# Decayed keys and queries by GpSimd, the first norm's sum kept in PSUM, and the keys' bias from eight more columns of the queries' product

## What is computed

```python
# tokens: softmax over the n = 16 pixels of a window, per head (8 heads of 8)
q = _ln(reduce_feats, ln_q_w, ln_q_b) @ Wq.T
kv = _ln(unf, ln_kv_w, ln_kv_b) @ Wkv.T
attn = softmax(einsum('bhpd,bhpnd->bhpn', q * scale, k), axis=-1)
aggre = einsum('bhpn,bhpnd->bhpd', attn, v)
h = reduce_feats + aggre @ proj_w.T + proj_b
# linear attention in chunks of 128 tokens, carried state S
scores = einsum('bhcd,bhed->bhce', qi, ki) * mask
intra = einsum('bhce,bhed->bhcd', scores, vi)
inter = einsum('bhcd,bhde->bhce', qi * q_dec, S)
S_new = blk * S + einsum('bhcd,bhce->bhde', ki * k_dec, vi)
# first norm over the 64 channels
h = _layernorm(h + attention(h))
```

## Time and profile before

| | us |
|---|---|
| median of three runs | 2586.48 (2584.95 to 2589.83) |
| the profiled execution, its own time | 2589.41 |
| its span | 2587.0 |
| first block's last norm starts (L929) | 2164.7 |

### The profile page before, as it was taken

One profiled execution on the slowest core, in us unless ns is written; L12 is line 12 of the kernel. 1 busy time (PEld: TensorE's weight loads), 2 busy tenths in 40 slices (PEclk: granted clock), 3 DMA queues, 4 the chain that ended last, 5 costly groups with the idle time before them and its releaser, 6 DMA issues. The chain is left out here.

```text
span 2587.0 us, 91002 instructions
## 1 busy us (share of the span) xinstructions
PE 2248.5 (87%) x32685; PEld 1057.8 (41%) x32685; DVE 2053.0 (79%) x3996; ACT 1851.1 (72%) x4405; POOL 1839.2 (71%) x1949
## 2 busy tenths in 40 slices
PE   1888898888888888888888888888888885999997
PEld 1344444444444444444444444444444442222222
DVE  4588888887888888888888888888888886777775
ACT  2877777777777777777777777777777773555554
POOL 3688788887888888888888888888888862233333
PEclk9999999999999999999999999999999996999999
DMA  4433333333333333333333333333333300010001
GB/s 79 83 67 67 66 66 66 67 66 57 64 67 67 67 67 67 67 67 67 67 67 67 67 67 67 67 67 67 67 67 67 67 2 1 17 23 22 20 20 29
DMA packets 573783, 147.92 MB, mean 57 GB/s; under 512 B 573504, under 2 KB 573504, under 8 KB 573504
## 3 DMA queue, kind: packets, MB, share of 16 engines
q1 hardware_dynamic: 573504, 143.53, 29.0%
HBM read 135.10 MB, written 8.39 MB: 55 GB/s over the span
## 5 line engine op out<-in xcount | busy, mean ns | idle before, releaser
L709 POOL TENSOR_TENSOR pv<-vs,aw 128x512 f32<-128x512 f32 x512 | 540.2, 1086 | 306.5 <-DVE aw L912 306.5
L856 DVE TENSOR_TENSOR kqs<-ps,qqT 128x512 f32<-128x512 f32 x512 | 354.1, 692 | 299.5 <-PE ps L393 295.2
L595 ACT ACTIVATE xd<-xb 128x512 f32<-128x512 f32 x512 | 585.4, 1178 | 0.0
L388 PE MATMUL ps<-xb,w_ckv 64*64 64x512 f32 x2048 | 555.6, 619 | 5.0 <-DVE kqs L856 5.0
L393 PE MATMUL ps<-xb,w_ckv 64*64 64x512 f32 x2048 | 555.6, 619 | 0.0
L577 ACT ACTIVATE sqs<-ps 128x512 f32<-128x512 f32 x512 | 308.4, 602 | 247.2 <-PE ps L393 246.9
L753 POOL TENSOR_TENSOR xt<-xb 128x512 f32<-128x512 f32 x256 | 325.8, 1273 | 23.0 <-issue 22.6
L716 POOL TENSOR_TENSOR pv<-pv 128x512 f32<-128x512 f32 x256 | 320.5, 1271 | 0.0
L867 DVE TENSOR_TENSOR sm<-ps,decay 128x1024 f32<-128x1024 f32 x256 | 299.5, 1208 | 4.4 <-PE ps L471 4.4
L415 PE MATMUL ps<-w_ckv,xd 64*64 64x64 f32 x16384 | 301.1, 223 | 0.0
L415 PEld LDWEIGHTS ps<-w_ckv,xd 64*64 64x64 f32 x16384 | 266.1, 136 | 33.1 <-issue 3.0
(11 more groups left out here) (223 smaller groups left out, 4261.6 us busy)
## 6 DMA issues: line engine op xcount, KB each, us to landing
xb<-in_x_dram SPq DMA_DIRECT2D x512, 256.0 KB, 4.4
out_dram<-outb SPq DMA_DIRECT2D x128, 64.0 KB, 1.6
w1p<-in_L_ffn_w_dram SPq DMA_DIRECT2D x16, 16.0 KB
w2p<-in_L_ffn_w_dram SPq DMA_DIRECT2D x8, 16.0 KB
b1p<-in_L_ffn_b_dram SPq DMA_DIRECT2D x8, 0.2 KB
b2v<-in_L_ffn_b_dram SPq DMA_DIRECT2D x8, 2.0 KB
sm<-in_L_tok_Wkv_dram SPq DMA_DIRECT2D x4, 16.0 KB, 2.0
w_av<-in_L_attn_w_qkv_dram SPq DMA_DIRECT2D x4, 16.0 KB, 2.1
```

What stands on the lines that cost most here:

```text
L388: nc.tensor.matmul(KB[own, :], w_ckv[own, 2 * P + m * C:2 * P + (m + 1) * C], xv[own, j], start=True, stop=True)
L595: nc.scalar.activation(xd[:, j, :].rearrange("p (b t) -> p b t", b=ST), xb[:, f, :].rearrange("p (b t d) -> p d b t", b=ST, d=ST)[:, j], A ...
L709: nc.gpsimd.tensor_tensor(pv[:, at].rearrange("p (k d) -> p k d", d=D), vs[:, s, at].rearrange("p (k d) -> p k d", d=D), aw[:, j * W4:(j + ...
L856: V.tensor_tensor(kqs[:, j, :].rearrange("p (t d) -> p t d", d=ST), KB.rearrange("p (t d) -> p t d", d=ST), qqT[:, s, :].unsqueeze(2).to_b ...
```

## The change

Three things, in the first block alone.

1. `kd` and `qdm` are made by GpSimd, behind `htok` and ahead of the sums of x, and no more by VectorE.
2. The sum `lt` stays in PSUM, as `LT`, 144 columns of bank B5 where L518's product lies: VectorE adds `htok` in place, ScalarE squares it there. The norm into `h1` is one product of 144 columns that reads `LT`; it stands right behind `q2` and waits for `oT`. L518 now waits for `h1`, and `attend(0)` waits for ScalarE's squares and no more for the sum. `sblk` stands ahead of the sum.
3. The keys' bias comes from the queries' product: `w_qc` has eight more columns, VectorE scales them by `yrs` and adds `cb_row` into `sbq`, which has four slots, twice behind `q2`. TensorE's product with `selbk` in `turned` is gone. `mx` and `mxb` are two columns of bank B4 in place of SBUF.

The diff's core:

```diff
-                                nc.tensor.transpose(SB[:, d * P:(d + 1) * P], sv[:, d, :], ident[:])
-                            nc.tensor.matmul(sgr[:, :, 25:26], qqT[:, o, :], selbk[:], start=True,
-                                             stop=True).then_inc(tr_pe, 1)
+                                mm = nc.tensor.transpose(SB[:, d * P:(d + 1) * P], sv[:, d, :], ident[:])
+                            mm.then_inc(tr_pe, 1)
...
-                                mm = nc.tensor.matmul(B67[:, m, 0:P], h1[own, 4 * i + r + 1, 0:P], w_qc[own, :],
+                                mm = nc.tensor.matmul(B67[:, m, 0:P + HEADS], h1[own, 4 * i + r + 1, 0:P], w_qc[own, :],
...
-                            pe.wait_ge(lt_done, done(i, r, 5, 1))
+                            pe.wait_ge(ln_sq, done(i, r, 5, 1))
...
+                            pe.wait_ge(h1_done, done(i, r, 5, 1))
+                            nc.tensor.matmul(LT, oT[:], w_ap[:], start=True, stop=True).then_inc(pr_done, 1)
...
+                        if s == 1:
+                            pool.wait_ge(st_ev, pairs(i, r, 0, 2))
+                            pool.wait_ge(s_pe, pairs(i, r, -1))
+                            nc.gpsimd.tensor_tensor(kd[:].rearrange("p (m h d) -> p m h d", m=2, d=D),
+                                                    kpl[:].rearrange("p (m h d) -> p m h d", m=2, d=D),
+                                                    kdec[:].unsqueeze(1).unsqueeze(3).to_broadcast([P, 2, HEADS, D]),
+                                                    ALU.mult).then_inc(kd_done, 1)
+                        else:
+                            pool.wait_ge(o_done, done(i, r, 5, 1))
+                            nc.gpsimd.tensor_tensor(qdm[:], qT[:, o, :], qdec[:], ALU.mult).then_inc(qd_done, 1)
...
                         V.tensor_tensor(heads(q2[:]), B67[:, :, 0:C], yrs[:, 2:4, 2:3].to_broadcast([P, 2, C]),
-                                        ALU.mult).then_inc(q2_done, 1)
+                                        ALU.mult)
+                        for m in range(2):
+                            ins = V.scalar_tensor_tensor(sbq[:, (r + 1) % 4, m * HEADS:(m + 1) * HEADS],
+                                                         B67[:, m, P:P + HEADS], yrs[:, 2 + m, 2:3],
+                                                         cb_row[:, m * HEADS:(m + 1) * HEADS], ALU.mult, ALU.add)
+                        ins.then_inc(q2_done, 1)
+                    if there(i, r, 5):
+                        dve.wait_ge(oT_done, done(i, r, 4, 1))
+                        V.tensor_tensor(h1[:, bass.ds(4 * i + r - 5, 1), :].rearrange("p o (m c) -> p (o m) c", c=CR),
+                                        LT.rearrange("p (m c) -> p m c", c=CR),
+                                        yrs[:, 0:2, 2:3].to_broadcast([P, 2, CR]), ALU.mult).then_inc(h1_done, 1)
...
-                        for m in range(2):
-                            ins = V.tensor_scalar(h1[:, bass.ds(4 * i + r - 5, 1), m * CR:(m + 1) * CR],
-                                                  lt[:, m * CR:(m + 1) * CR].unsqueeze(1), yrs[:, m, 2:3], None, ALU.mult)
-                        ins.then_inc(h1_done, 1)
...
-                        V.tensor_tensor(lt[:], B5[:, P:P + 2 * CR], htok[:, s, :], ALU.add).then_inc(lt_done, 1)
...
+                        V.tensor_tensor(LT, LT, htok[:, s, :], ALU.add).then_inc(lt_done, 1)
```

More of the change, by code:

```diff
@@ L98, in vit_tower_kernel @@
         B5 = ps[:, 5, :]
+        LT = B5[:, P:P + 2 * CR]
         B6 = ps[:, 6, :]
@@ L113, in vit_tower_kernel @@
         selbk = sb("selbk", [P, SL])
-        w_qc = sb("w_qc", [P, P])
+        w_qc = sb("w_qc", [P, P + HEADS])
+        cb_row = sb("cb_row", [P, SL])
         w_pj = sb("w_pj", [P, P])
@@ L171, in vit_tower_kernel @@
             eps_c = sb1("eps_c", [P, 1])
-            mxb = sb1("mxb", [P, SL])
             sb2 = sb1("sb2", [P, SL])
             aw = sb1("aw", [P, N * SL])
-            mx = sb1("mx", [P, SL])
+            sbq = sb1("sbq", [P, 4, SL])
             den = sb1("den", [P, SL])
@@ L331, in _ @@
                     nc.tensor.transpose(ps[:, 0, j * P:(j + 1) * P], cat[:, j, :], ident[:])
+                nc.tensor.matmul(ps[:, 5, 0:SL], cat[:, 0, :], selbk[:], start=True, stop=True)
+                nc.tensor.matmul(ps[:, 5, SL:2 * SL], scr[:, 0, :], selbk[:], start=True, stop=True)
                 for j in range(2):
@@ L618, in step @@
                         for m in range(2):
-                            ins = squares(lt[:, m * CR:m * CR + C], ssq[:, m:m + 1], l2[:, m * C:(m + 1) * C])
+                            ins = squares(LT[:, m * CR:m * CR + C], ssq[:, m:m + 1], l2[:, m * C:(m + 1) * C])
                         ins.then_inc(ln_sq, 1)
@@ L896, in step @@
                     sn = sgr[:, :, 0:SL]
+                    mx, mxb = [sgr[:, :, c:c + 1].rearrange("p n w -> p (n w)") for c in (25, 26)]
                     s4 = sn.rearrange("p n (m h) -> p n m h", h=HEADS)
@@ L926, in step @@
                                                ALU.add, ALU.add).then_inc(hT_done, 1)
-                    if there(i, r, 5):
-                        for m in range(2):
-                            ins = V.tensor_scalar(h1[:, bass.ds(4 * i + r - 5, 1), m * CR:(m + 1) * CR],
-                                                  lt[:, m * CR:(m + 1) * CR].unsqueeze(1), yrs[:, m, 2:3], None, ALU.mult)
-                        ins.then_inc(h1_done, 1)
-                    if there(i, r, 3) and s == 1:
-                        dve.wait_ge(st_ev, pairs(i, r, 0, 2))
-                        dve.wait_ge(s_pe, pairs(i, r, -1))
-                        V.tensor_tensor(kd[:].rearrange("p (m h d) -> p m h d", m=2, d=D),
-                                        kpl[:].rearrange("p (m h d) -> p m h d", m=2, d=D),
-                                        kdec[:].unsqueeze(1).unsqueeze(3).to_broadcast([P, 2, HEADS, D]),
-                                        ALU.mult).then_inc(kd_done, 1)
-                    if there(i, r, 3) and s == 0:
-                        dve.wait_ge(o_done, done(i, r, 5, 1))
-                        dve.wait_ge(qk_ev, done(i, r, 3, 2))
-                        V.tensor_tensor(qdm[:], qT[:, o, :], qdec[:], ALU.mult).then_inc(qd_done, 1)
                     if there(i, r, 4):
                         dve.wait_ge(pr_done, done(i, r, 4, 1))
-                        dve.wait_ge(h1_done, done(i, r, 5, 1))
                         dve.wait_ge(hb_done, done(i, r, 4, 1))
-                        dve.wait_ge(ln_sq, done(i, r, 5, 1))
                         if s == 0:
                             dve.wait_ge(s_pe, pairs(i, r, -1))
-                        V.tensor_tensor(lt[:], B5[:, P:P + 2 * CR], htok[:, s, :], ALU.add).then_inc(lt_done, 1)
-                        if s == 0:
                             dve.wait_ge(o_done, done(i, r, 5, 1))
```

14 lines of the change are left out of this document (8 added, 6 removed).

## The result

The changed kernel takes **2468.6 us** (median of 4 runs, 2467.3 to 2469.9) against 2585.7 (4 runs, 2582.6 to 2589.8): ratio 0.9545, interval 0.9534 to 0.9557. The profiled execution has a span of 2466.0 us, 121.0 less than before. Forecast were 2480 us and 107 less.

A forecast was written before the change was run, and what follows sets the result against it. The prediction took TensorE's L456, waiting for VectorE's mask, as the bound. Saving 3.51 us in four steps over 30.75 turns, 108 us, plus 1 of setup, gave 2480 us by the median; range for 8 in 10: 2443 to 2508.

The forecast's parts named there:

- The bound of the kernel before: TensorE's L456 waits for VectorE's mask, which is late by VectorE's queue; the wait costs 1.46 us a step.
- K: Start of the fourth keys product on VectorE (L856, j = 3), from which times in a step are measured.
- What is late next: ScalarE ends kT at K+5.20, so L456 starts at K+5.3 in place of K+6.27.
- GpSimd holds the second keys product by 0.2 us: GpSimd's pv delays agg to K+8.1 and that product to K+10.22; TensorE alone would be ready at K+10.02.
- A, C and D: Of four successive steps A, B, C, D, one turn of the hardware loop, lasting 16.30, 15.63, 17.34 and 15.52 us.
- The other signs that were named: Profile after: mask near K+3.5, L456 idle under 0.5 us, released by ScalarE, kd and qdm about 0.4, four steps 61.3.
- What was taken away in C: Second keys product in step C moves from K+12.03 to K+10.22, saving 1.81 us.
- The price of the removed instructions: L929 twice and L942 or L935, between hT and the mask on VectorE: 2.4 us in A, 0.7 more in C.
- GpSimd's new work: kd or qdm once a step on GpSimd, behind htok: 0.41 us as L737, costed at nothing.
- The short slot behind q2: VectorE's new work there was costed at nothing; the rival, chance 0.20, had the slot too short: +18 us, 2498.
- TensorE as the only bound (0.12): Rival, chance 0.12: pv comes 0.2 to 0.35 us sooner, second keys product at K+10.02 in each step, 2455 us.
- GpSimd as a bound that makes it slower (0.03): Rival, chance 0.03: kd and qdm on GpSimd cost above 1.9 us; at 2.5, 0.6 a step, about 2662 us.

The follow-up runs named there:

- e5: Changed kernel with ScalarE's last gather, gather(3, 0), moved behind all the copies, just ahead of centred(0): 2449.7 us.
- e6: Changed kernel with one spare 128x128 product on GpSimd between the four pieces of pv and their sums: 2487.7 us.
- e9: e1 with one more 128x128 product from SBUF directly behind each decay product on VectorE: 2471.5 us.
- e2: Kernel before with only the decay products kd and qdm moved to GpSimd: 2504.4 us.
- e7: Changed kernel with one spare 128x128 product on GpSimd behind htok: 2468.9 us.
- e1: Changed kernel with the decay products kd and qdm back on VectorE, between hT and the sum: 2469.2 us.
- e4: Changed kernel with ScalarE's gather(3, 0) behind the copies qT and kT in place of ahead of them: 2478.3 us.
- e10: e5 and e1 together, the gather behind the copies and the decay products on VectorE: 2454.2 us.
- e8: Kernel before with one useless TensorE product of 128 by 512 columns ahead of L456's wait: 2578.2 us.

## Why the prediction was right, and where it was off

**The bound of the kernel before** (the mask late by VectorE's queue, L456 behind it): right. With the instructions gone the mask starts at K+3.80, forecast K+3.75.

**What is late next:** right as to who, ScalarE's kT. kT is done at K+5.22 (forecast K+5.20), but L457 starts 0.25 us after that and not 0.1, at K+5.47 in place of K+5.3. The 0.1 for a signal was an assumption and is mis-sized: the start of a TensorE product behind the end of ScalarE's copy took 0.25 us.

**GpSimd holds the second keys product by 0.2 us, at K+10.22 in all four steps:** this is the step of the sum that failed, in its reason. In the kernel after it comes at K+10.20, 10.07, 10.22 and 10.03. agg does wait for pv in each kind of step, but by 0.14 to 0.18 us in the medians and not by 0.3 to 0.5, and in A, C and D that wait is not what holds the product. There the product waits for TensorE once agg is done, 0.21 us in A and C and 0.07 in D (medians); in A it is 4.73 us behind L457, the 4.72 of the forecast. Only in B does it follow agg at once, 1.89 us behind agg's start. I had taken 2.12 for that from B of the kernel before, where no wait is reported: 0.13 us lay between agg's end and the product all the same. So pv alone would allow the product at K+8.00+1.89 = K+9.9, 0.3 under the forecast's K+10.22, and TensorE alone, in A, at K+5.47+4.72 = K+10.2, 0.2 over the forecast's K+10.02. The later of the two decides, and so the number in A and C came out right with the wrong engine behind it, by luck; B and D come 0.15 and 0.19 before it. Together 0.02+0.15+0+0.19 = 0.36 us a turn, 11 us over the kernel. e5 and e6 show both limits from either side: take away ScalarE's 0.3 and pv holds, delay pv by 0.4 and half of it is lost.

**The other signs that were named:** the mask was put near K+3.5 there and at K+3.75 in the working, it came at K+3.80; L456 was to idle under 0.5 us, it idles 0.60; ScalarE as its releaser, 0.4 us for kd and qdm, and GpSimd idle before pv (0.88 us in A) came as said; four steps last 60.9 and not 61.3 us.

**What was taken away in C:** 1.81 us, right in the typical turn (1047.38 was K+12.03; now K+10.22). The second term that was missing are the six long steps, 10 us, which I hadn't seen because I read one turn and took it for all; the lowered clock stands in the windows view. The span fell by 14 us more than forecast (121.0 for 107), and that is 11 and 10 from these two terms, less 2.5 behind the last weights and 4 in the steps at both ends.

**The price of the removed instructions:** I wrote that their prices "are not those of the work", and that held, 2.4 us in A. What I missed is how it is made up. In A of the kernel before the two L929 took 0.25 and 1.11 us; this is the tile view of that line from 1003 to 1006 us (shortest, median and longest in ns, first and last start):

```profile
L929 DVE TENSOR_SCALAR h<-lt,yrs x2: 249/682/1114, 1005.6 to 1005.8; 128x72 f32 x2
```

With L942's 1.21 they end one by one behind the pieces of pv; a first such instruction is nearly free, and with the scores coming some 1.4 us behind hT two of them cost next to nothing in A (e9, mask at K+4.00; e2, K+4.01 in the median). It is the third that costs there. C is another case, where hT came 0.3 us later against pv. The first L929 there, from the kernel before:

```profile
1037.89 0.96 DVE L929 TENSOR_SCALAR h<-lt,yrs 128x72 f32 x1
```

pv had begun at 1036.68; with pieces of 1.05 us its first gap, at 1037.73, had passed when L929 started, and it had to wait for the next, at 1038.77. It ends at 1038.85. So the long step C hung on 0.16 us. e2 keeps these two instructions, and its C keeps the 2.00 us.

The prediction had the second instruction wait for the whole of the other engine's; these rows show it waiting for the rest of the piece that runs, so that the price depends on where in the piece it starts.

**GpSimd's new work:** 0.41 us was taken from L737. The group by line and form of the kernel after, 1000 to 1260 us:

```profile
L742 POOL TENSOR_TENSOR qdm<-qT,qdec 128x128 f32<-128x128 f32 x9 | 4.2, 462 | 0.0
L736 POOL TENSOR_TENSOR kd<-kpl,kdec 128x128 f32<-128x128 f32 x8 | 3.3, 408 | 0.0
```

0.41 and 0.46, and at no cost: 0.4 us more changes nothing either (e7), and neither does taking the product back to VectorE (e1). The Trainium skill's rule ("GPSIMD Engine Reference", 3.1 Elementwise: about one cycle an element on VectorE, 2.6 on GpSimd) has the right direction, 0.41 to 0.46 us against 0.28 for L935 with GpSimd idle, but it decides nothing here, since both places are free.

**The short slot behind q2:** the rival with 0.20 did not come. The two groups of the kernel after:

```profile
L910 DVE SCALAR_TENSOR_TENSOR sbq<-ps,yrs,cb_row 128x8 f32<-128x8 f32 x34 | 5.9, 217 | 0.0
L916 DVE TENSOR_TENSOR h<-ps,yrs 128x144 f32 x17 | 5.2, 307 | 0.8 <-ACT oT L657 0.6
```

The two small ones take 0.35 as a pair, for 0.30 assumed, and in B the third keys product follows h at once, 2.24 us behind the second, for 2.26 before. The cover was as thin as I had it, and held. TensorE as the only bound (0.12) is true of A, C and D and not of B, and without the earlier pv on which I had hung it: its four pieces became 0.05 us shorter in A and not 0.2 to 0.35. GpSimd as a bound that makes it slower (0.03): e7 shows 0.4 us more to cost nothing.

## What to carry to other kernels

Read the shortest and the longest of a repeated step over the whole trace before one is taken as typical; the rare long ones were 10 of the 121 us here. Where two engines share a way into SBUF, count the instructions that stand in a row beside the other's long ones, not their lengths: the first may be nearly free and each further one cost a whole piece of the other. After the bound was taken away the next two lay within 0.3 us of each other, and moving one small block off the way of all copies (e5) gave more than moving it off one (e4), which lost.

## What the runs showed of the hardware

- VectorE's instructions with all their inputs in SBUF (L929, L935, L942 and the like) get in behind the end of a piece of pv on GpSimd, one for each end. In the records of the full steps the blocked ones end 0.05 to 0.06 us behind it (L929) or 0.15 (the products). With pieces of 1.05 to 1.07 us that makes 0.25 to 0.45 us for a first one shortly ahead of such an end, 1.1 to 1.2 for each that follows, and 0.96 for a first one that has missed it. It costs the other side little: four pieces of pv take 4.18 us with no such instruction beside them and 4.19 with two L929 (e2), 4.24 with one product (e1, e10) and 4.29 with two (e9).
- TensorE's granted clock fell to its lower level, 1.2 of 2.4 GHz, behind idle times of 2.3 us in six of some thirty turns with the same idle time, and behind 1.5 us in five (e2). In the full steps it did not fall once where the idle time was 0.6, or where 1.1 us of useless products went into the 2.3 (e8). What picks the turns is open.
- On VectorE the instruction of 8 columns from PSUM (L910) takes 0.217 us, that of 48 columns 0.21 (L903) and that of 144 columns 0.31 (L916): from 8 to 48 columns the size does not show.
